# Two gated attention and expert layers on one core: the first k projection moved ahead of the first q, one normalization moved to ScalarE, slot numbers of one chunk moved a step, and the waits between the first layer's experts and the second layer moved

## The reference, cut to what matters

```python
x = x + tanh(g_xattn[0]) * L0_xattn(layernorm(x), ctx)       # 16 heads of 16, 128 keys per batch
x = x + tanh(g_ffn[0])   * L0_ffn(layernorm(x))              # 8 experts, top 1, capacity 1.5, gelu
x = x + tanh(g_xattn[1]) * L1_xattn(layernorm(x), ctx, ctx)
x = x + tanh(g_ffn[1])   * L1_ffn(layernorm(x))              # 4 experts, all computed, top 2 mixed

# attention: q from x, k and v from ctx, softmax(q k^T / 4) v, times W_proj
# L0_ffn: a token goes to expert e = argmax(x @ router_w.T); its place is a running count
pos  = cumsum(onehot)[token, e] - 1;  kept = pos < C
buf[e, min(pos, C-1)] += x * kept                             # C = 1536
y = eo[e, min(pos, C-1)] * (softmax probability * kept)       # eo = gelu(buf w1 + b1) w2 + b2
```

## Time and profile before

| | |
|---|---|
| median of 3 runs | 2127.8 us (2127.56 to 2128.17) |
| the profiled execution | 2127.45 us |
| its span, first to last instruction | 2125.5 us |
| TensorE matmul busy | 2024.2 us (95%) |
| TensorE weight load busy (beside the matmuls) | 1773.9 us (83%) |
| VectorE busy | 1791.5 us (84%) |
| ScalarE busy | 1482.0 us (70%) |
| GpSimd busy | 1203.1 us (57%) |
| granted TensorE clock, mean | 0.985 of full speed |

### The profile page before, as it was taken

One profiled execution on the slowest core, in us unless ns is written; L12 is line 12 of the kernel. 1 busy time (PEld: TensorE's weight loads), 2 busy tenths in 40 slices (PEclk: granted clock), 3 DMA queues, 4 the chain that ended last, 5 costly groups with the idle time before them and its releaser, 6 DMA issues.

```text
span 2125.5 us, 57374 instructions
## 1 busy us (share of the span) xinstructions
PE 2024.2 (95%) x19532; PEld 1773.9 (83%) x19532; DVE 1791.5 (84%) x4918; ACT 1482.0 (70%) x3172; POOL 1203.1 (57%) x1736
## 2 busy tenths in 40 slices
PE   6999999999699999999699999999999999999997
PEld 5878888888599999999678888888788888888885
DVE  5898998988588888888588888887689999999996
ACT  4766666666378787878466666666678888888885
POOL 5788888787300000000277777777457777777776
PEclk9999999999799999999899999999999999999998
DMA  7565222221366666666422222222101110001000
GB/s 231 176 195 175 69 61 70 65 63 45 133 235 227 243 226 244 224 246 222 159 84 70 74 69 75 70 76 76 34 26 31 31 31 30 30 30 31 31 28 18
DMA packets 168047, 226.09 MB, mean 106 GB/s; under 512 B 20454, under 2 KB 152170, under 8 KB 157420
## 3 DMA queue, kind: packets, MB, share of 16 engines
q1 hardware_dynamic: 161644, 205.99, 29.2%
q0 software_dynamic: 6144, 16.79, 2.6%
HBM read 153.77 MB, written 68.94 MB: 105 GB/s over the span
## 4 chain that ended last, share of the span: by engine, by line
PE 83%; DVE 8%; issue 4%; POOL 2%; DMA 1%; ACT 1%; SPq 0%; POOLq 0%; DVEq 0%; ACTq 0%
PE ps L1279 11%; PE ps L1295 10%; PE ps L1041 10%; PE ps L1000 8%; PE ps L1127 5%; PE ps L1081 4%; PE ps L1227 4%; PE ps L1148 3%; PE ps L1239 3%; PE ps L1158 3%; PE ps L1181 3%; PE ps L1060 3%; DVE nmax L1432 2%; PE ps L1075 2%; PE ps L1098 2%
## 5 line engine op out<-in xcount | busy, mean ns | idle before, releaser
L1432 DVE TENSOR_REDUCE nmax<-ps 128x16 f32<-128x2048 f32 x128 | 292.5, 2285 | 30.6 <-PE ps L1098 30.2
L889 ACT ACTIVATE prob_t<-ps 128x2048 f32<-128x2048 f32 x128 | 240.8, 1881 | 105.2 <-PE ps L1081 105.2
L694 POOL COPY slot_in<-slot_all 128x1 int32<-128x1 int32 x64 | 13.2, 207 | 473.0 <-DMA eo_d<-eo 473.0
L1041 PE MATMUL ps<-w2f,a_t 128*128 128x256 f32 x1024 | 231.7, 379 | 0.3 <-ACT a_t L811 0.3
L1279 PE MATMUL ps<-xgt_hi,w_hl 128*128 128x256 f32 x1248 | 230.3, 283 | 1.0 <-DVE xgt_lo L1699 1.0
L1295 PE MATMUL ps<-w_hl,hid_hi 128*128 128x256 f32 x1248 | 226.8, 283 | 0.0
L1041 PEld LDWEIGHTS ps<-w2f,a_t 128*128 128x128 f32 x1024 | 189.6, 190 | 23.8 <-ACT a_t L811 0.6
L961 ACT ACTIVATE hid<-ps,b_in 128x256 f32<-128x256 f32 x312 | 146.1, 469 | 82.6 <-PE ps L1279 67.3
L1279 PEld LDWEIGHTS ps<-xgt_hi,w_hl 128*128 128x128 f32 x1248 | 195.5, 189 | 1.4 <-issue 1.4
L811 ACT ACTIVATE a_t<-ps,be_in,g_in 128x128 f32<-128x128 f32 x512 | 186.0, 470 | 12.3 <-PE ps L1060 11.3
L668 POOL TENSOR_TENSOR km_r<-k_in,cst 128x512 fp32r<-128x512 f32 x128 | 134.8, 1053 | 102.8 <-ACT k_in L869 102.7
(11 more groups left out here) (237 smaller groups left out, 6345.3 us busy)
## 6 DMA issues: line engine op xcount, KB each, us to landing
w_raw<-in_w_dram SPq DMA_DIRECT2D x78, 1024.0 KB, 6.8
c_t<-in_ctx_in_dram SPq DMA_DIRECT2D x128, 128.0 KB
x_d<-x SPq DMA_DIRECT2D x128, 128.0 KB, 1.7
slots_d<-zeros SPq DMA_DIRECT2D x12, 1024.0 KB, 5.6
eo_d<-zeros SPq DMA_DIRECT2D x12, 1024.0 KB, 5.5
xg<-slots_d SPq DMA_DIRECT2D x39, 256.0 KB, 2.7
eo_d<-eo SPq DMA_DIRECT2D x39, 256.0 KB, 2.2
x_in<-in_x_dram SPq DMA_DIRECT2D x64, 128.0 KB
```

What stands on the lines that cost most here:

```text
L889: nc.scalar.activation(prob_t[:].rearrange("p a k -> p (a k)"), scores.rearrange("p a k -> p (a k)"), ACT.Exp, scale=SOFT).then_inc(y["exp ...
L1041: mm = pe.matmul(dst, a_t[:, b.parity, e, c, :], w2f[:, e, c, :], start=False, stop=True, skip_group_check=True)
L1432: nc.vector.tensor_reduce(nmax[:, b.parity, :, 0:4], scores.rearrange("p a (r k) -> p a r k", k=P), AX_X, ALU.max, negate=True).then_inc(y ...
```

## The change

- `QK_AT` and `PROB_AT` move by 4 words, `slot_in` becomes a buffer of its own for the whole program, `rs2` grows to 128 x 3.
- k of batches 0 and 1 is computed in step -1, in front of the transposition of xh of batch 1 and the first q, and copied out there; step 0 has no k any more. The first q waits for `k_out`. This holds for both attention loops.
- `xh2` is computed by ScalarE: `x1 * rs2 + (-mean * rs2)`, queued behind `o_pad` and ahead of `c_hi`, `k_in` and `v_aug`. VectorE computes the 128 x 1 factor `-mean * rs2` in the place of the old instruction, as a third step of `n2_rstd`.
- The eight slot instructions of the chunk of batch 56 stand in step 67, right behind that chunk's `den8`. All others stay.
- In GpSimd's step 67 (the last with an `o_lo`), `o_lo` comes ahead of the second `rstd`.
- SyncE no longer waits for the landing of the last `eo_d` stores; GpSimd waits for it behind the first `slot_in` copy, just ahead of the first gather.

```diff
-    QK_AT, PROB_AT = 11022, 15630
+    QK_AT, PROB_AT = 11018, 15626
+        slot_in = sb("slot_in", [P, 4, 1], I32)
-        slot_in = psb("slot_in", [P, 4, 1], I32)
-        rs2 = psb("rs2", [P, 2])
+        rs2 = psb("rs2", [P, 3])
-                 ... n2_rstd=2, ...
+                 ... n2_rstd=3, ...
@@ SyncE, end of stage 2
-                    for g in (NH - 2, NH - 1):
-                        sp.wait_ge(z["eo_stored"].of(At(0, g)), z["eo_stored"].at(At(0, g)))
@@ GpSimd, step
+                    def low_part():
+                        b = s - 4
+                        if b.within(B):
...
+                            nc.gpsimd.tensor_tensor(o_lo[:, b.parity], o_t[:, b.parity], o_hi[:, b.parity], ALU.subtract)\
+                                .then_inc(y["o_lo_done"].sem, 1)
+                    if (s - 4).within(B) and not (s - 3).within(B):
+                        low_part()
+                        second_rstd()
+                    else:
+                        second_rstd()
                     b = s + 5
                     if n == 1 and b.within(B):
...
                         pool.wait_ge(y["slot_read"].of(b), y["slot_read"].at(b))
+                        if b.off == 0:
+                            for g in (NH - 2, NH - 1):
+                                pool.wait_ge(z["eo_stored"].of(At(0, g)), z["eo_stored"].at(At(0, g)))
...
+                    if not ((s - 4).within(B) and not (s - 3).within(B)):
+                        low_part()
@@ GpSimd, end of stage 1
-                    for g in (NH - 2, NH - 1):
-                        pool.wait_ge(z["eo_stored"].of(At(0, g)), z["eo_stored"].at(At(0, g)))
@@ ScalarE, step, behind o_pad
+                    b = s - 5
+                    if n == 0 and b.within(B):
+                        act.wait_ge(y["n2_rstd"].of(b), y["n2_rstd"].at(b))
+                        if (b - 8).begun:
+                            act.wait_ge(y["scattered"].of(b - 8), y["scattered"].at(b - 8))
+                        nc.scalar.activation(xh2[:, b.off % 8, :], x1[:, b.off % 4, :], ACT.Identity, scale=rs2[:, 1:2], bias=rs2[:, 2:3])\
+                            .then_inc(y["xh2_done"].sem, 1)
@@ ScalarE and TensorE, k
-                    e = s
-                    if e.off % 2 == 0 and e.within(B):
+                    e = s + 1 if s.off == -1 else s
+                    if s.off != 0 and e.off % 2 == 0 and e.within(B):
@@ TensorE, ahead of q
-                        if s.off >= 0 and s.off % 2 == 0:
+                        if s.off == -1:
+                            pe.wait_ge(y["k_out"].of(s + 2), y["k_out"].at(s + 2))
+                        elif s.off > 0 and s.off % 2 == 0:
                             pe.wait_ge(y["k_out"].of(s + 1), y["k_out"].at(s + 1))
@@ VectorE, step
                     b = s - 5
                     if n == 0 and b.within(B):
-                        dve.wait_ge(y["n2_rstd"].of(b), y["n2_rstd"].at(b))
-                        if (b - 8).begun:
-                            dve.wait_ge(y["scattered"].of(b - 8), y["scattered"].at(b - 8))
-                        nc.vector.tensor_scalar(xh2[:, b.off % 8, :], x1[:, b.off % 4, :], mv2[:, 0:1], rs2[:, 1:2], ALU.subtract, ALU.mult)\
-                            .then_inc(y["xh2_done"].sem, 1)
+                        dve.wait_ge(y["n2_rstd"].of(b), y["n2_rstd"].at(b, 2))
+                        nc.vector.tensor_scalar(rs2[:, 2:3], mv2[:, 0:1], rs2[:, 1:2], -1.0, ALU.mult, ALU.mult).then_inc(y["n2_rstd"].sem, 1)
...
                     b = s - 12
-                    if n == 0 and b.off % CH == 0 and b.within(B):
+                    if n == 0 and b.off % CH == 0 and b.within(B) and b.off != B - 2 * CH:
+                        slots_from_places(b)
...
                         nc.vector.tensor_reduce(den8[:], ex8[:], AX_X, ALU.add).then_inc(st.sem, 1)
+                        if b.off == B - 2 * CH:
+                            slots_from_places(b)
...
+                        if n == 0 and (b - 4).begun:
+                            dve.wait_ge(y["xh2_done"].of(b - 4), y["xh2_done"].at(b - 4))
```

More of the change, by code:

```diff
@@ L395, in flamingo_gated @@
                  av_done=1, o_pad_done=1, o1_done=1, o_norm=2, o2_done=1, o_t_done=2, o_lo_done=1, pr_done=1, res_biased=1, x1_done=1,
-                 n2_stats=2, n2_rstd=2, xh2_done=1, x2_turned=1, x2_t_done=1, lg_done=1, lg_read=1, top_steps=5, ex_done=1,
+                 n2_stats=2, n2_rstd=3, xh2_done=1, x2_turned=1, x2_t_done=1, lg_done=1, lg_read=1, top_steps=5, ex_done=1,
                  cum_done=1, cum_read=2, slots_steps=12))
@@ L684, in step, with second_rstd @@
                         rstd(y["n1_stats"], mv1, rs1, y["n1_rstd"], b)
[L685 to L689, removed]
+                    def second_rstd():
+                        b = s - 5
+                        if n == 0 and b.within(B):
+                            if (b - 1).begun:
+                                pool.wait_ge(y["xh2_done"].of(b - 1), y["xh2_done"].at(b - 1))
+                            rstd(y["n2_stats"], mv2, rs2, y["n2_rstd"], b)
+                    def low_part():
+                        b = s - 4
+                        if b.within(B):
+                            pool.wait_ge(y["o_t_done"].of(b), y["o_t_done"].at(b))
+                            if (b - 2).begun:
+                                pool.wait_ge(y["pr_done"].of(b - 2), y["pr_done"].at(b - 2))
+                            nc.gpsimd.tensor_tensor(o_lo[:, b.parity], o_t[:, b.parity], o_hi[:, b.parity], ALU.subtract)\
[5 more added lines that the diff above has]
+                        second_rstd()
                     b = s + 5
@@ L1443, in step, with slots_from_places @@
                     if n == 0 and b.within(B):
-                        dve.wait_ge(y["n2_rstd"].of(b), y["n2_rstd"].at(b))
-                        if (b - 8).begun:
-                            dve.wait_ge(y["scattered"].of(b - 8), y["scattered"].at(b - 8))
-                        nc.vector.tensor_scalar(xh2[:, b.off % 8, :], x1[:, b.off % 4, :], mv2[:, 0:1], rs2[:, 1:2], ALU.subtract, ALU.mult)\
-                            .then_inc(y["xh2_done"].sem, 1)
[L1449 to L1456, removed]
-                    if n == 0 and b.off % CH == 0 and b.within(B):
+                        dve.wait_ge(y["n2_rstd"].of(b), y["n2_rstd"].at(b, 2))
+                        nc.vector.tensor_scalar(rs2[:, 2:3], mv2[:, 0:1], rs2[:, 1:2], -1.0, ALU.mult, ALU.mult).then_inc(y["n2_rstd"].sem, 1)
+                    def slots_from_places(b):
                         c = chunk(b)
@@ L1475, in step @@
                         dve.wait_ge(st.of(c), st.at(c, 12))
+                    b = s - 1
+                    if b.within(B):
+                        dve.wait_ge(y["max_turned"].of(b), y["max_turned"].at(b))
+                        if (b - 2).begun:
+                            dve.wait_ge(y["s2_done"].of(b - 2), y["s2_done"].at(b - 2))
+                        nc.vector.tensor_tensor(nmax_x[:, b.parity], b7[:, 0:P].unsqueeze(1).to_broadcast([P, 4, P]),
+                                                row_mask.unsqueeze(2).to_broadcast([P, 4, P]), ALU.mult).then_inc(y["nmax_done"].sem, 1)
+                    b = s - 12
+                    if n == 0 and b.off % CH == 0 and b.within(B) and b.off != B - 2 * CH:
+                        slots_from_places(b)
                     b = s - 11
```

## The result

The changed kernel takes 2165.8 us (median of 4 runs, 2165.3 to 2167.0); the kernel before, on the same chip, 2128.0 (4 runs, 2127.6 to 2128.4). The ratio is 1.018, 95% interval 1.016 to 1.020. I had forecast 2111, in 2103 to 2124, with 0.11 for slower. The profiled execution has a span of 2163.7 us, 38.2 more than before.

A forecast was written before the change was run, and what follows sets the result against it. Stage 1 looked TensorE-bound, but once in four steps TensorE waited behind VectorE, and VectorE behind GpSimd; borders also bound. Steady 13.9 (18.9 - 5) + 1.2 + 0 + 1.5 = 16.6 us, from 2127.8 to 2111.2, range 2103 to 2124.

The forecast's parts named there:

- The price of the rows on ScalarE: Stage 1: the new ScalarE instruction makes `x2_t` late in some steps, 0.09 us a step, 5 us (0 to 16.5).
- my 14 chunks: Stage 1: the fourteen four-step cycles inside the loop, each to gain 1.35 us, 18.9 us together.
- The gain: Stage 1 loop: VectorE, relieved of the second rows, no longer late with `o_n`; 18.9 us, lower bound 0.
- the collision: Once in four steps VectorE's slot instructions meet GpSimd's `km_r` and `c_lo`, taking 3.1 us from `far` to `slot_s`.
- the stall: TensorE's wait for VectorE's `o_n` at the 8.97 us step, 10.1 us in 12 waits from 100 to 500 us.
- The small factor: Stage 1: VectorE's new 128 x 1 instruction, forecast to take 0.21 us at most, with no wait for GpSimd.
- the slower rival: Stage 1: the factor waits for GpSimd in 28 odd steps, 1.0 us each, 28 us: 2134 us, chance 0.11.
- First k ahead of the first q: Start of the first attention loop: k's matmuls fill TensorE's wait for the second `xh`; gain 1.2 us (0.3 to 2.0).
- Slots of batch 56 and `o_lo` first: End of stage 1: four scatters ready earlier only wait for the last chunk's slots; gain 0 us (-0.3 to 0.9).
- Stage 2 to 3: Border: earlier loads and gather, k before q; gain 1.5 us (0.5 to 2.8); L1541 of batch 4 late next, moving 0.4.
- ScalarE's queue takes the gain back: Rival: `x2_t` 0.3 us late in each step leaves a steady part of 2.4 us: 2123 us, chance 0.17.
- The stall stays: Rival: `km_r` still meets the slot instructions, only the borders gain, 2.7 us: 2125 us, chance 0.10.

The follow-up runs named there:

- the rows last and the slots first: Changed kernel with ScalarE's second rows (xh2) behind the exponential and the eight slot instructions ahead of `nmax_x` on VectorE: 2110.4 us, ratio 0.9922.
- the 12 buffers: Changed kernel with 12 row buffers instead of 8, so the rows wait for the scatter of b-12, not b-8: 2139.8 us, ratio 1.006.
- the fast kernel: Changed kernel with ScalarE's rows behind the exponential and the slot instructions ahead of `nmax_x`: 2110.4 us, ratio 0.9922.
- rows last: Changed kernel with ScalarE's rows moved from ahead of `c_hi` and `k_in` to behind the exponential, same instruction and waits: 2126.4 us, ratio 0.9993.

## Why the prediction was wrong, point by point

**The price of the rows on ScalarE: wrong, and the step that failed.** I had 5 us. The changed kernel and the one with the rows last and the slots first both have the chunk's step at 7.8 us, and differ by 55.4 us (2165.8 and 2110.4; 53.9 if each is taken against the kernel before of its own group): that is the price, in four parts.
- *Left out: the wait for the scatter.* I named what is queued behind the new instruction, `c_hi`, `k_in`, `x2_t` and the exponential, and held against it ScalarE's time and the factor. I didn't ask what else the instruction waits for. Its second wait, for the scatter of eight batches before, moved with it. The row of before had the warning: 1.5 us of idle for `slots_d` in the earlier trace rows. On VectorE the rows don't hold up `k_in`; on ScalarE they do, and with it `km_r` and the next scatter. By the 12 buffers this is 26.0 us, with TensorE's fall to the lower clock in it, which the sum left out as well.
- *The wrong first user of `x2_t`.* "TensorE wants it at 276.38", L1205. The working up to there held: I had `x2_t` start 1.78 us after the end of `xh`, and in the kernel with 12 buffers it is 1.66 (294.68 to 296.34). But TensorE needs it earlier, at L1181, whose matmuls write the bank that `x2_t` is read from. In the trace of before it starts at 275.89 (row below), half a us ahead of L1205; in the changed kernel it is L1198, and in the one with 12 buffers it waits for `x2_t` 19.9 us in 37 waits from 100 to 500 us. Instead of just in time, `x2_t` is 0.4 late by my own sum. Steps 12 to 64 take 432.4 us with 12 buffers and 411.5 in the fast kernel: 20.9, or 0.40 a step where I had taken "0.09 a step".
- *The same in steps 1 to 12*, which my 14 chunks left out: 85.6 us with 12 buffers, 81.5 in the fast kernel, 4.1.
- *Not seen: the end of stage 1.* It is 41.6 us with 12 buffers and 37.0 in the fast kernel, 4.6. The last four scatters only wait for their slots, as I had it, but these start 35.9 us after the last step's first matmul in the changed kernel, for 30.8 before. I read it as the later `x2_t` and factor of the last batches passing through to them; no run tests that alone.

26.0 + 20.9 + 4.1 + 4.6 is 55.6. That it meets 55.4 so closely is in part chance, as the first is a difference of medians and the others are from one trace each. The row of TensorE in the kernel before that I should have taken for the deadline:

```profile
275.89 0.66 PE L1181 MATMUL ps<-cst,o_pad 128*128 128x128 f32 x4
```

**The gain: right in size, wrong in its reason.** I gave 18.9 us, from `far` being through before `km_r`. In the changed kernel and in the one with 12 buffers `far` is at 0.17 and the chunk's step at 7.8, and `k_in` is the 0.7 later that I gave it: it starts 0.61 us behind `nmax_x` (302.01 and 301.40), where before it started 0.06 ahead of it. But this rested on "`k_in` becomes later", the very delay that I priced at almost nothing. Gain and price were two ends of one delay: where the rows do no harm (rows last), `k_in` isn't later, the collision stays, and so does the stall. VectorE's relief alone bought nothing, as it stood ahead of a wait for TensorE. Slots ahead of `nmax_x` removed the collision itself, and brought 9 to 16 us.

**The small factor: right.** It takes 0.20 to 0.21 us in all 56 steps that the trace of the changed kernel has from 60 to 560 us, never behind GpSimd, so the slower rival was not the one that came. In 27 of them GpSimd was in the middle of an operation of 0.74 to 1.09 us (`km_r`, `o_lo` or the bias addition). The Trainium skill (SBUF — State Buffer, section "Who interferes with whom") has it that a VectorE instruction with at most one input in SBUF does not contend with GpSimd outside the two-port modes. The traces agree, if the factor, one element wide, is such a one, which no run here shows by itself; `far`, four wide, has a mean of 891 ns in the kernel with the rows last.

**First k ahead of the first q: right in kind, and the match of 1.2 us is luck.** The first step of the changed kernel starts 1.2 us earlier, but that is the least of eleven kernels with this edit: they start it at 20.5 to 22.2 us, the three without at 23.4 to 23.8. The edit alone has 2.3 in its trace and 2.5 in its medians. The q that I gave 1.8 us at a lower clock took 1.86 (at 18.00) and the next one 1.06, though the granted clock reads 1.00 over both.

**Slots of batch 56 and `o_lo` first: right by itself.** With the rows last, four early scatters end at 560.1 and then GpSimd waits 2.4 us for the last chunk's slots: no gain, as forecast.

**Stage 2 to 3: 1.5 forecast, 0 seen.** The load of `x_in` comes 1.7 us earlier against the first `xg`, but L1563 still waits for the gather of `y_in` (4.6 us, for 4.2 in the earlier trace rows), and the fourth step of the second loop is no earlier. The line I had named as late next was the bound: counted from the first load of `xg` it starts for batch 4 0.4 us later than before, and not 0.4 earlier.

**The rivals.** "ScalarE's queue takes the gain back" was the right mechanism at less than a third of its price, 16.5 us for 55; its end of 0.3 late in each step was no upper bound, since it was drawn from the margin to the wrong line, and knew no loop. "The stall stays" is what the rows last show.

## What to carry to other kernels

When an instruction moves to another in-order queue, list every one of its waits, and for each ask whether what it waits for is released, however indirectly, by something that now stands behind it. If so, a wait that was hidden becomes a loop, and any slow DMA in it is paid more than once: in the wait itself, in what is queued behind it, and in TensorE's clock, which fell here behind a wait of 3.08 us. Take a buffer's deadline from the first instruction that waits on its semaphore, which may only reuse the same PSUM bank. And put small work into a gap in which the engine waits anyway: it pays more than removing work ahead of a wait.

## What the runs showed of the hardware

- A scatter of 128 rows of 1 KB lands 2.5 us after its issue on the median. Issued within 0.3 us of a 1 MB fill on another queue, six took 5.2 to 6.5 us (12 buffers); behind the last fill they took up to 4.6 us (rows last).
- Behind a wait of 3.08 us TensorE's granted clock fell to 0.51 for the next 5.8 us, in which it was busy throughout (143.60 to 149.42, changed kernel).
- ScalarE's 128x256 rows, from one SBUF buffer to another with scale and bias from SBUF, take 0.60 us, and add 0.51 to the queue (294.83 to 295.34, 12 buffers). The estimate of 0.40 from the Trainium skill (VectorE: DVE Perf Modes, "The TRN2 errata"), weighed in the prediction, is not borne out.
- Eight VectorE instructions of 128x4 take 0.8 us together when GpSimd is quiet (rows last, slots first), and 3.4 us when they meet its `km_r`, `qm` and `c_lo` (306.20 to 309.58, rows last).
